# The beginning, the second-layer halves and the end of an attention and expert kernel, on one core

## The reference, cut to what matters

```python
x = x + xattn(ctx, _layernorm(x))        # 32 batches of 128 tokens, 256 wide, 16 heads of 64
x = x + ffn(_layernorm(x))

def xattn(x, latents, ...):              # x: the context, latents: the normed tokens
    x = layer_norm(x, ln_m_g, ln_m_b); lat = layer_norm(latents, ln_l_g, ln_l_b)
    q = lat @ Wq                         # 256 x 1024
    k, v = split(concatenate([x, lat], axis=1) @ Wkv)      # 256 keys a batch
    return softmax(q k^T / 8) v @ Wout

def ffn(x, centroids, ln_g, ln_b, w1, b1, w2, b2):         # 8 experts, 256 -> 1024 -> 256
    assign = argmax(x @ centroids.T)     # one expert a token
    y = x + relu(xn @ w1[e].T + b1[e]) @ w2[e].T + b2[e]
    return a * y + (1 - a) * x           # a = sigmoid of the chosen affinity
```

## Time and profile before

| | |
|---|---|
| median of 3 runs | 1091.27 us (1089.54 to 1091.3) |
| profiled execution | 1091.64 us, span 1089.8 us |
| busy share of the span | PE 98%, PEld 87%, DVE 73%, ACT 61%, POOL 47% |
| PE busy in 0 to 20 us / 20 to 40 / 40 to 60 | 14.88 / 16.46 / 17.05 us |
| PE busy in 200 to 800 us | 600.00 us |
| PE busy in 1060 to 1080 us / 1080 to 1090 | 17.20 / 0.00 us |
| chain that ended last | PE 93% |

### The profile page before, as it was taken

One profiled execution on the slowest core, in us unless ns is written; L12 is line 12 of the kernel. 1 busy time (PEld: TensorE's weight loads), 2 busy tenths in 40 slices (PEclk: granted clock), 3 DMA queues, 4 the chain that ended last, 5 costly groups with the idle time before them and its releaser, 6 DMA issues.

```text
span 1089.8 us, 24096 instructions
## 1 busy us (share of the span) xinstructions
PE 1063.2 (98%) x8508; PEld 953.5 (87%) x8508; DVE 790.3 (73%) x1873; ACT 662.0 (61%) x1819; POOL 515.8 (47%) x640
## 2 busy tenths in 40 slices
PE   7899999999999999999999999999999999999995
PEld 6689888989888888989898888889898999999994
DVE  5786888888888988888887988888975543333331
ACT  4674766575756767665767667665665555555540
POOL 1563555546464555546464645555345533332331
PEclk9998999999999999999999999999999999999998
DMA  5465576765857566766758576765468466556540
GB/s 167 116 159 158 145 194 163 189 170 145 216 139 199 148 182 163 190 164 170 182 150 209 150 187 148 188 167 130 101 174 291 143 209 234 207 201 241 198 158 23
DMA packets 152172, 187.11 MB, mean 172 GB/s; under 512 B 16621, under 2 KB 141549, under 8 KB 147184
## 3 DMA queue, kind: packets, MB, share of 16 engines
q1 hardware_dynamic: 147600, 175.68, 58.7%
q0 software_dynamic: 3360, 8.53, 2.2%
q10 hardware_dynamic: 1088, 1.31, 0.3%
HBM read 65.72 MB, written 46.07 MB: 103 GB/s over the span
## 4 chain that ended last, share of the span: by engine, by line
PE 93%; DVE 2%; POOL 1%; DMA 1%; ACT 1%; issue 1%; SPq 0%; ACTq 0%; POOLq 0%; DVEq 0%
PE psum L661 16%; PE psum L694 15%; PE psum L836 12%; PE psum L731 11%; PE psum L821 10%; PE psum L710 9%; PE psum L746 9%; PE psum L680 8%; PE psum L749 1%; PE psum L789 1%; DMA w_ring<-in_w_q 1%; POOL prob L1583 1%; DMA prob_t<-prob 1%; DVE neg_max L1221 0%; POOL w_o_lo L1637 0%
## 5 line engine op out<-in xcount | busy, mean ns | idle before, releaser
L1583 POOL TENSOR_TENSOR prob<-prob,inv_sum 128x512 f32<-128x512 f32 x176 | 182.8, 1053 | 206.0 <-DVE inv_sum L1227 205.5
L990 ACT ACTIVATE prob<-psum,neg_max 128x256 f32<-128x256 f32 x352 | 164.3, 479 | 47.9 <-DVE neg_max L1221 40.4
L1221 DVE TENSOR_REDUCE neg_max<-psum 128x2 f32<-128x512 f32 x256 | 162.2, 673 | 34.9 <-PE psum L710 34.7
L836 PE MATMUL psum<-w,v_n 128*128 128x256 f32 x608 | 134.2, 379 | 0.0
L1233 DVE STREAM_TRANSPOSE prob<-prob 128x512 f32<-128x512 f32 x176 | 121.5, 699 | 9.5 <-POOL prob L1583 8.9
L836 PEld LDWEIGHTS psum<-w,v_n 128*128 128x128 f32 x608 | 114.1, 190 | 14.8
L1654 POOL DMA_INDIRECT out<-x_in,r_ring x38 | 47.5, 1250 | 152.2 <-DVE x_in L1452 146.4
L1583 POOL TENSOR_TENSOR w_ring<-w_ring,inv_sum 128x512 f32<-128x512 f32 x76 | 78.2, 1042 | 78.0 <-DVE inv_sum L1227 77.7
L997 ACT ACTIVATE head_out_hi<-psum 128x512 fp32r<-128x512 f32 x52 | 31.1, 598 | 114.6 <-PE psum L731 107.7
L969 ACT ACTIVATE k_hi<-psum 128x512 fp32r<-128x512 f32 x128 | 77.2, 603 | 22.9 <-PE psum L661 19.3
L980 ACT ACTIVATE v_n<-psum 128x512 f32<-128x512 f32 x128 | 78.2, 611 | 20.9 <-PE psum L694 20.9
(11 more groups left out here) (183 smaller groups left out, 2712.1 us busy)
## 6 DMA issues: line engine op xcount, KB each, us to landing
sorted_rows<-filler SPq DMA_DIRECT2D x54, 660.0 KB, 5.0
prob_t<-prob SPq DMA_DIRECT2D x176, 128.0 KB, 2.8
w_ring<-prob SPq DMA_DIRECT2D x176, 128.0 KB
w<-in_experts SPq DMA_DIRECT2D x19, 1024.0 KB
w_ring<-in_experts SPq DMA_DIRECT2D x18, 1024.0 KB, 6.0
prob_t<-w_ring SPq DMA_DIRECT2D x76, 128.0 KB, 2.8
w_ring<-w_ring SPq DMA_DIRECT2D x76, 128.0 KB
w_ring<-normed SPq DMA_DIRECT2D x56, 128.0 KB, 3.0
```

The costliest lines, as they stand in the source:

```text
L836: last = pe.matmul(bank[:, i * d_model:(i + 1) * d_model], hid[:, s % 2, f, i * P:(i + 1) * P], w2[:, f * d_model:(f + 1) * d_model], star ...
L990: act.activation(prob_at(u, bb)[:, :, parity, i], scores_i, ACT.Exp, bias=neg_max[:, at, i:i + 1], accum_out=prob_sum[:, at, i:i + 1]).the ...
L1221: dve.tensor_reduce(neg_max[:, (4 * u + n) % 8, :], psum[:, n, :].rearrange("p (i j) -> p i j", i=2), AXIS_X, ALU.max, negate=True).then_i ...
L1583: pool.tensor_tensor(probs, probs, inverse, ALU.mult).then_inc(s_soft, 1)
```

## The change

It has three parts.

**The beginning.** The norm of the first pair is done a side at a time: variances, power and shifts of side 0 are made before the statistics of side 1 are through (`first_variances`, `first_shifts`, `first_normalised` in place of `first_scales`), on a semaphore of its own (`s_lnp_first`). ACT normalises side 0 ahead of the high part of the first query weights. The high parts of the inputs are made straight from PSUM, by gain and bias with an fp32r output, ahead of `y_t`; the two copies go. The first keys are done pass by pass over both banks instead of bank by bank; one of three blank products goes. One product of values stands between queries and scores, two behind the scores, one behind the queries of step 1. DVE makes the low part of `V_FIRST` ahead of the first low keys, and that of `Q_FIRST` behind the inputs.

**The halves.** `layer_2` puts each half into a bank of its own and tells of each; `finish` takes them singly. `bank_order` gets an item more a slot, and items called "pass" that skip a bank, so that every slot uses the same three banks.

**The end.** POOL waits in each slot from slot 6 on until that slot's rows have landed and then executes a `drain()`. The branches of the slots that may be empty are nested, so that the first empty one leaves them all, and the eight branches at the end go.

```diff
-    order += [("rank", n_pairs - 2), ("ft", 1), ("fy", 0), ("pv", n_steps - 1), ("wout", n - 2), ("ft", 2), ("wout", n - 1)]
+    order += [("rank", n_pairs - 2), ("ft", 1), ("fy", 0, 0), ("fy", 0, 1), ("pv", n_steps - 1), ("wout", n - 2), ("ft", 2), ("wout", n - 1)]
...
-        order += [("ft", slot + 2)] * (slot + 2 < n_slots) + [("fy", slot)]
+        order += [("ft", slot + 2) if slot + 2 < n_slots else ("pass", slot, 0), ("fy", slot, 0), ("fy", slot, 1), ("pass", slot, 1)]
...
                 def layer_2(s):
-                    bank = begin(("fy", s))
...
                     for i in range(2):
+                        bank = begin(("fy", s, i))
                         for f in range(FC):
...
-                            last = pe.matmul(bank[:, i * d_model:(i + 1) * d_model], hid[:, s % 2, f, i * P:(i + 1) * P],
+                            last = pe.matmul(bank[:, 0:d_model], hid[:, s % 2, f, i * P:(i + 1) * P],
...
-                    last.then_inc(f_y, 1)
+                        last.then_inc(f_y, 1)
...
-                warm(3)
-                first_keys(0)
-                first_keys(1)
+                warm(2)
+                first_keys()
                 weights_split(Q_FIRST)
                 queries(0)
+                weights_split(V_FIRST)
+                values(0, 0, 0)
...
                     scores(u)
                     if u == 0:
-                        weights_split(V_FIRST)
-                        for bb in range(2):
-                            for side in range(2):
-                                values(0, bb, side)
+                        values(0, 0, 1)
+                        values(0, 1, 0)
                         weights_split(K_REST)
...
                         values(*item[1:])
+                    if u == 0:
+                        values(0, 1, 1)
...
                 high_weights(K_FIRST)
+                normalise(0)
                 high_weights(Q_FIRST)
-                normalise(0)
                 act.wait_ge(s_early, 2 * 16)
+                first_inputs()
                 gain_bias(0, 0)
-                wait_read(act, ("ln", 0, 0))
-                act.activation(kv_t[0][:, :, 0:2, 0:P], y_t[:, :, :, 0:P], ACT.Copy).then_inc(s_hi_first[0], 1)
                 high_weights(V_FIRST)
...
+                def first_variances(side):
+                    part = slice(2 * side, 2 * side + 2)
+                    var = mean_var[:, part, 1]
+                    dve.wait_ge(s_mv, 2 * side + 2)
...
                     for c in range(KC):
-                        last = dve.tensor_scalar(y_t[:, c, :, P:2 * P],
-                                                 work_bank(number[item])[:, 2 * c * P:2 * (c + 1) * P].rearrange("p (b t) -> p b t", b=2),
-                                                 ln_w[:, 2, c:c + 1], ln_w[:, 3, c:c + 1], ALU.mult, ALU.add)
+                        last = dve.tensor_scalar(kv_t[0][:, c, 0:2, P:2 * P], raw[c], ln_w[:, 2, c:c + 1], ln_w[:, 3, c:c + 1],
+                                                 ALU.mult, ALU.add)
+                    last.then_inc(s_hi_first[1], 1)
+                    for c in range(KC):
+                        last = dve.tensor_scalar(y_t[:, c, :, P:2 * P], raw[c], ln_w[:, 2, c:c + 1], ln_w[:, 3, c:c + 1],
+                                                 ALU.mult, ALU.add)
                     last_reads(item, last)
+                    wait_high(dve, 0, 1)
                     wait_read(dve, item)
-                    dve.tensor_copy(kv_t[0][:, :, 0:2, P:2 * P], y_t[:, :, :, P:2 * P]).then_inc(s_hi_first[1], 1)
-                    wait_high(dve, 0, 1)
...
-                    last_reads(item, dve.tensor_tensor(upd, work_bank(number[item]).rearrange("p (i d) -> p i d", i=2),
-                                                      b2_ring[:, s % NR, None, :].to_broadcast([P, 2, d_model]), ALU.add))
...
                     for i in range(2):
+                        item = ("fy", s, i)
+                        wait_made(dve, item)
+                        last_reads(item, dve.tensor_tensor(upd[:, i, :], work_bank(number[item])[:, 0:d_model],
+                                                          b2_ring[:, s % NR, :], ALU.add))
...
-                pool.wait_ge(s_var, 1)
-                pool.tensor_tensor(ln_scale[:, 0, :], var_eps[:], minus_half[:], ALU.pow).then_inc(s_pow, 1)
+                for side in range(2):
+                    part = slice(2 * side, 2 * side + 2)
+                    pool.wait_ge(s_var, side + 1)
+                    pool.tensor_tensor(ln_scale[:, 0, part], var_eps[:, part], minus_half[:, part], ALU.pow).then_inc(s_pow, 1)
...
-                for s in range(n_early, n_slots):
-                    run(s + 2, (add_base,))
-                    run(s, (write_rows,))
-
-                for s in range(n_sure - 1, n_slots):
-                    with pool.If(empty == n_slots - 1 - s):
-                        for i in range(2):
-                            pool.wait_ge(f_out[(s - i) % 2], 32 * ((s - i) // 2 + 1))
+                pool.wait_ge(f_out[(n_early - 2) % 2], 32 * ((n_early - 2) // 2 + 1))
+                pool.wait_ge(f_out[(n_early - 1) % 2], 32 * ((n_early - 1) // 2 + 1))
+                pool.drain()
+                with ExitStack() as inner_blocks:
+                    for s in range(n_early, n_slots):
+                        if s >= n_sure:
+                            inner_blocks.enter_context(pool.If(empty < n_slots - s))
+                        run(s + 2, (add_base,))
+                        write_rows(s)
+                        pool.wait_ge(f_out[s % 2], 32 * (s // 2 + 1))
+                        pool.drain()
```

## The result

| | before | changed |
|---|---|---|
| median | 1090.4 us (1088.03 to 1091.3, 4 runs) | 1076.2 us (1073.96 to 1077.15, 4 runs) |
| ratio | | 0.987, 95% interval 0.9847 to 0.9894 |
| profiled execution / span | 1091.64 / 1089.8 us | 1075.77 / 1073.9 us |
| PE's last product ends | 1077.2 | 1069.0 |
| last indirect DMA ends | 1081.6 | 1071.7 |

The change is faster by 14.2 us, medians against medians, and by 15.9 us between the two profiled executions. The forecast was 12.7 less, 1078.6.

A forecast was written before the change was run, and what follows sets the result against it. PE, busy 600.00 of 600.00 us between 200 and 800, bounds the kernel; only its beginning and end can move. 5.5 + 1.6 + 0.3 + 5.3 = 12.7 us less gives 1078.6 by the median, range 1075.0 to 1084.8.

The forecast's parts named there:

- First keys 11.3, first scores 17.7: Beginning on PE: first keys start at 11.3 instead of 16.05, first scores at 17.7, 4.2 us earlier.
- the third pass: First keys' third pass needs both low parts and waits for POOL's, which costs 0.5 us.
- The port: Beginning: DVE with two SBUF inputs shares a port with POOL; POOL's subtraction would end at 13.8, not 13.5.
- 5.5 carried into the stretch without gaps: Low part of `V_REST` at 30.5, 5.5 us earlier; DVE is last and passes this on; bounds 3 and 6.5.
- The clock: Rival: the clock loss of 3.4 us between 84 and 96 us falls differently; none lost gives 1075.2, or more; 6%.
- The halves, 1.6: Behind PE's end: last DMA ends 2.76 us after PE instead of 4.38, 1.6 saved; slots cost 0, at most 1.
- The drain, 5.3: End of POOL: the 5.80 us drain shrinks because its price grows with DMAs since the last one; 5.3 us saved.
- The linear reading of two points: POOL's drains of 0.17 us (no DMA) and 5.80 (70 DMAs) read as 0.080 us for each DMA.
- The flat drain: Rival: a drain costs the same whenever a DMA came before; 5.5 us less gain, 1084.1; 20%.
- the slower rival: Rival: the drain is longer than POOL's slot allows, about 7 us free; at 9 us the time is 1100; 5%.
- The branches, 0.3: End, between last DMA and drain: the branches go, saving 0.3 us of at most 0.6.

The follow-up runs named there:

- The beginning alone: The kernel before with only the new beginning put in: median 1084.39 us, ratio 0.9945.
- the end alone: The kernel before with only POOL's new end (waits for the slot's writes and a drain in every late slot): median 1082.52 us, ratio 0.9939.
- the halves alone: The kernel before with only the halves of the second layer in own banks, added, scaled and written singly: median 1087.28 us, ratio 0.9975.
- more warming: The kernel before with 13 warming products ahead of the first transposes instead of 9: median 1089.81 us, ratio 1.0.

## Why the prediction was right

- **First keys 11.3, first scores 17.7**: 11.32 and 17.43. The chain was right in its order, though not each link: POOL's first power took 0.72, not 1.0, its second 1.14, and the query weights landed before 8.31, not at 9.44. The beginning alone had them at 9.52: first keys 11.42, a wait of 0.59 on the third pass (0.5 predicted), scores 18.20, half a microsecond later than written. PE kept a gap over 1 us, 1.40 ahead of the first transposes (8.54), where the prediction had none.
- **The port.** I let POOL's subtraction be lengthened, to 13.8. POOL took its 1.30 as ever; DVE paid. The rows of the beginning alone:

```profile
12.11 1.30 POOL L1615 TENSOR_TENSOR kv_t_lo<-y_t,kv_t_hi 128x512 fp32r<-128x512 f32 x1 [3.58 <-ACT y_t L971]
...
12.33 1.63 DVE L1293 TENSOR_TENSOR kv_t_lo<-y_t,kv_t_hi 128x512 fp32r<-128x512 f32 x1
```

  DVE's ends 0.55 behind POOL's end there, 0.54 in the changed kernel (13.19 and 12.65), and before's copy ended 0.54 behind POOL's (15.95 and 15.41): it did its work when POOL was through. The rule of the Trainium skill ("SBUF — State Buffer", "Who interferes with whom") that one of the two waits whole agrees with the two subtractions. The same section leaves it to the order of issue which one, and so do these rows: POOL was first in all three (by 0.88, 0.22 and 0.13 us), and DVE waited. The prediction read `L1261` as such a case of two inputs; it is a copy with one input, of which that rule says nothing. What counted was its place: ahead of POOL's subtraction it took 0.43 and not 1.68 (the end alone, above).
- **5.5 carried into the stretch without gaps**: 6.5 between the profiles, 5.84 at the low part of `V_REST`. The term was near the truth of these two executions by luck. I read the first keys at 16.05, the copy's 1.68 and the transposes' 1.94 us as the kernel's, when the granted clock over 8 to 16 us was 0.79. Against other executions of the same beginning it is 3.2 to 4.8, so 5.5 was 0.7 to 2.3 us too much. The 6.5 at the centroid products is nearer to what PE's queries of step 1 gained (6.39) than to DVE's 5.84, which I had as the last; which of the two carries isn't shown.
- **The clock** stood among the rivals at 6%, as a way for 84 to 96 us to fall differently. It did: 1.7 of the 3.2 us by which the profiled difference exceeds the forecast. The rest is 1.0 at the beginning and 0.4 in the branches (the drain and the halves came as said). The rule on idle gaps in the Trainium skill ("TensorE: Matmul & The Clock Gate", "Why this matters for your kernels") was set aside there, and rightly: PE is busy 22.00 of 22.00 us at 0.84.
- **The halves, 1.6**: 1.62, and no cost in the slots.
- **The drain, 5.3**: 5.3. The linear reading of two points was right; now six points lie on it. The flat drain (20%) is out, and with it the slower rival: the longest drain of the changed kernel is 3.67 us, ahead of the slots, and those in them 0.2.
- **The branches, 0.3**: 0.7. The five branches behind the landing take 0.05 us each but start from 1083.0 to 1083.7, some 0.17 apart; I counted their durations, not their distances.

The medians fell by 14.2, and by 13.3 when both were measured again (1089.71 to 1076.45). Parts that the traces show whatever the clock does, 3.2 to 4.8, 1.6, 0.7 and 5.3, make 10.8 to 12.4. The rest may be the clock, which loses less in the changed kernel by the means of the whole executions (0.998 against 0.992); that is argued, not shown. The half clock at before's end (0.63 granted over 1080 to 1090 us, where PE has no work) explains some of that difference in the mean clock but none of the time. How much of the gain the clock is by medians stays open. So the total came near in part by luck: a beginning taken too large stood in for a gain from the clock that the sum did not count.

## What to carry to other kernels

Before a beginning is read from one profile, look at the granted clock and at the waits on DMAs in it: other executions of the same code had the first scores 2 us earlier. A drain of POOL costs by the indirect DMAs issued since the last one (0.082 us each), so a drain put where POOL is idle takes the price off the end. Look for every wait that a piece of work can fill, not only the first: two products of values, put into a wait of 1.51 and one of 2.03 a step later, brought the second scores 2.25 us forward, where the first product alone is worth about 1.4.

## What the hardware showed unexpectedly

- POOL's DRAIN: 0.04 us and 0.082 us for each indirect DMA since the last drain, though all of these had landed (5.80 behind 70).
- 1.2 GHz is granted to a PE without idle time (22.00 of 22.00 us busy at 0.84 and 0.92): in 12 of 14 profiles the clock fell around the 8-column products, and halving these or mixing them with 512-column ones did not stop it. That these products bring it about isn't shown, since none was run without them. The other two (the halves alone and more warming) kept 1.00 there and had their half clock near 34 us, behind a wait of 2.03; they are also the two whose query weights are seen to land before 7 us, a link that no run tests. The same code showed either, so one execution doesn't tell.
- DVE's copy of 128x512 took 0.43 us when it started ahead of POOL's subtraction and 1.68 when it started 0.13 behind it.
- The DMA of the first query weights landed between 6.6 and 9.5 us in different executions (ACT's wait on it ended at 6.57, 6.64, 8.71, 8.77, 9.44 and 9.52).
